# Attention's result in fp32, the first mixture's first layer on 64-row tiles, the loop written out, and new instruction orders

## The reference

```
x = x + attention(ln_c(x))          # q, k, v; softmax over d of q, over n of k; context; Wout
t = t + LN(moe0(ln_t(t)) + ln_t(t)) # router per IMAGE: mean of tokens, top 2 of 8 experts, gelu
x = x + conv3x3(ln_c(x), sign weights x mean|w|)
t = t + moe1(ln_t(t))               # all 8 experts, gelu, weighted per TOKEN by its top 2 gates
```

## Time and profile before

| | us |
|---|---|
| median of 3 runs | 429.95 (429.81 to 431.31) |
| profiled execution, whole | 429.15 |
| its span, first to last instruction | 427.4 |
| PE busy | 367.0 (86%) |
| DVE busy | 298.1 (70%) |
| ACT busy | 256.2 (60%) |
| POOL busy | 102.2 (24%) |

### The profile page before, as it was taken

How to read it: one execution, slowest core, us unless ns; L and a number is a source line. 1 busy time by engine, 2 the same in 40 slices (tenths; PEclk the granted TensorE clock), 3 DMA queues, 4 the chain that set the end, 5 groups by cost and what they waited for, 6 DMA issues and landing times.

```text
span 427.4 us, 6147 instructions
## 1 busy us (share of the span) xinstructions
PE 367.0 (86%) x1847; PEld 197.8 (46%) x1847; DVE 298.1 (70%) x691; ACT 256.2 (60%) x521; POOL 102.2 (24%) x93
## 2 busy tenths in 40 slices
PE   3869889899817465789999999999999998999994
PEld 3457676777704244354454444444444433433321
DVE  2498889998541545748778778778788788577442
ACT  2346557585635524458678678678678557557543
POOL 5226465656610313013013013012022021010000
PEclk9699999999966966679999999999999999999999
DMA  6930000000000000000010010010010010010101
GB/s 152 175 100 7 9 34 2 2 2 1 2 1 0 2 0 1 0 0 2 1 26 1 0 26 1 2 25 1 0 25 0 0 25 2 0 25 2 25 2 26
DMA packets 15947, 7.46 MB, mean 17 GB/s; under 512 B 14160, under 2 KB 14416, under 8 KB 15920
## 3 DMA queue, kind: packets, MB, share of 16 engines
q1 hardware_dynamic: 15920, 7.13, 8.4%
HBM read 5.03 MB, written 2.10 MB: 17 GB/s over the span
## 4 chain that ended last, share of the span: by engine, by line
PE 59%; DVE 17%; issue 11%; ACT 6%; POOL 2%; DMA 2%; POOLq 0%; ACTq 0%; DVEq 0%; SPq 0%
PE ps L787 13%; PE ps L816 11%; PE ps L739 6%; PE ps L694 4%; PE ps L797 4%; PE ps L709 3%; ACT HB L1432 2%; DVE qsum L995 2%; PE ps L615 2%; PE ps L763 2%; PE ps L808 1%; PE ps L527 1%; PE ps L574 1%; PE ps L724 1%; POOL rstdA L444 1%
## 5 line engine op out<-in xcount | busy, mean ns | idle before, releaser
L1226 DVE TENSOR_TENSOR XC<-HB,ps 128x512 f32<-128x512 f32 x128 | 83.6, 683 | 44.5 <-PE ps L797 26.4
L1432 ACT ACTIVATE HB<-ps,B1B 128x512 f32<-128x512 f32 x128 | 82.3, 683 | 42.6 <-PE ps L787 40.7
L787 PE MATMUL ps<-ET,W1B 64*128 64x512 f32 x256 | 71.1, 632 | 3.5 <-ACT HB L1432 3.0
L816 PE MATMUL ps<-XC,W2B 128*64 128x512 f32 x256 | 67.2, 613 | 0.4 <-DVE XC L1226 0.4
L444 POOL TENSOR_TENSOR rstdA<-varA,pow_half 128x8 f32<-128x8 f32 x16 | 26.2, 1638 | 139.4 <-DVE varA L917 139.4
L797 PE MATMUL ps<-CWTB,SEL 64*128 64x512 f32 x128 | 36.8, 570 | 2.6 <-DVE XC L1226 2.6
L444 POOL TENSOR_TENSOR rstd<-var,pow_half 128x4 f32<-128x4 f32 (+1 forms) x24 | 29.4, 1229 | 30.8 <-DVE var L917 30.3
L787 PEld LDWEIGHTS ps<-ET,W1B 64*128 64x128 f32 x256 | 20.6, 187 | 28.2 <-ACT HB L1432 15.3
L444 POOL TENSOR_TENSOR rstdB<-varB,pow_half 128x8 f32<-128x8 f32 x8 | 13.1, 1637 | 84.5 <-DVE varB L917 84.5
L739 PE MATMUL ps<-VP,WC 128*128 128x512 f32 x96 | 30.6, 478 | 1.5 <-ACT CWTB L1425 0.8
L694 PE MATMUL ps<-UTR,W1S 128*128 128x512 f32 (+1 forms) x64 | 24.7, 488 | 6.8 <-ACT XC L1380 3.8
(11 more groups left out here) (221 smaller groups left out, 656.2 us busy)
## 6 DMA issues: line engine op xcount, KB each, us to landing
out<-W1stage SPq DMA_DIRECT2D x8, 256.0 KB, 2.9
XC<-in_x SPq DMA_DIRECT2D x6, 256.0 KB, 5.7
T<-in_x SPq DMA_DIRECT2D x1, 512.0 KB, 3.7
W1stage<-in_w1a SPq DMA_DIRECT2D x1, 512.0 KB
W1B<-in_w1b SPq DMA_DIRECT2D x1, 512.0 KB, 3.6
W1stage<-in_wconv SPq DMA_DIRECT2D x1, 288.0 KB, 2.7
W1stage<-in_wcs SPq DMA_DIRECT2D x1, 288.0 KB, 3.1
K<-in_consts SPq DMA_DIRECT2D x1, 266.0 KB, 2.8
```

Of the source, the lines that this page charges most:

```text
L787: mm(ps[:, H_BANK[c], :], W1B[half(c), e, :], ET[half(c), par, :], start=True, stop=True).then_inc(s["f_h"], 1)
L816: ins = mm(acc[c * C:(c + 1) * C, :], W2B[:, e, :], HG[:, (2 * e + c) % 4, :], start=False, stop=(e == E - 1), skip_group_check=True)
L1226: tt(HG[:, m % 4, :], HB[:, m % 2, :], ps[:, CW_BANK[m % 2], :], ALU.mult).then_inc(s["f_hg"], 1)
L1432: av(HB[:, m % 2, :], ps[:, H_BANK[m % 2], :], ACT.Gelu, bias=B1B[:, m // 2:m // 2 + 1])\
```

## The change

- The kernel keeps attention's result in fp32 only. `u_to_channels` is now two fp32 products of 128 x 129 in place of four fp32r transposes; its extra column is of ones and gives the sum over tokens. ACT copies it in one instruction into `UT`, where four had done copy and sum. The cast (DVE) and the subtraction (POOL) are gone.
- The first layer of the first mixture is multiplied in fp32 on 64-row tiles: `a_hidden` has 2 parts with 2 products each, one on the upper 64 rows of the array and one on the lower. They write two banks (A and V). The preparation of a split W1 is gone. The tokens of a unit are g and g+4 in place of neighbours.
- All periods are written out; there is no hardware loop.
- Both tables of orders are new.

```diff
 PLAN = dict(
     pool=(
-        "b_rstd-1 a_rstd1 a_rstd0+1"
+        "a_rstd0+2 a_rstd1+2 b_rstd+2"
...
-def periods(eng, plan, parts):
+def periods(plan, parts):
...
-    for b in range(-MOST_AHEAD, MOST_AHEAD):
-        period(b, b % 2, plan, parts, image_exists)
-    with eng.Fori(0, (B - 2 * MOST_AHEAD) // 2) as i:
-        for par in range(2):
-            period(eng.snap(2 * i + (MOST_AHEAD + par)), par, plan, parts, lambda name, b, ahead: True)
-    for b in range(B - MOST_AHEAD, B + MOST_AHEAD):
+    for b in range(-MOST_AHEAD, B + MOST_AHEAD):
         period(b, b % 2, plan, parts, image_exists)
...
-        W1A = sb("W1A", [P, E, 2, F], F32R)
+        W1A = sb("W1A", [P, E, F])
...
-            return (H_BANK + CW_BANK)[n] if early(b) else A_BANK
+            return (H_BANK + CW_BANK)[n] if early(b) else (A_BANK, V_BANK)[n % 2]
...
             def u_to_channels(g):
...
-                    pe.wait_ge(s["ulo"], n + 1)
+                    pe.wait_ge(s["u"], n + 1)
...
-                    for r in range(4):
-                        ins = pe.transpose(ps[:, UT_BANK, r * P:(r + 1) * P].bitcast(F32R),
-                                           US[:, n % 2, r].rearrange("p k c -> p (k c)"), ident_r[:, :])
+                    for i in range(2):
+                        ins = mm(ps[:, UT_BANK, i * (P + 1):(i + 1) * (P + 1)],
+                                 U[:, 2 * p + i, UT_ * g:UT_ * g + UT_, :].rearrange("p h c -> p (h c)"), IDS[:, :],
+                                 start=True, stop=True)
...
-            def a_hidden(n):
+            def a_hidden(k):
                 def part(b, par):
-                    k, c = n // 2, n % 2
-                    if c == 0:
-                        pe.wait_ge(s["a_sel"], 4 * b + 2 * k + 1)
+                    pe.wait_ge(s["a_sel"], 4 * b + 2 * k + 1)
                     if early(b):
-                        ge(pe, s["a_gelu"], 4 * (b - 1) + n + 1)
-                    elif n == 0:
-                        ge(pe, s["a_z"], b)
+                        ge(pe, s["a_gelu"], 4 * (b - 1) + 2 * k + 2)
+                    elif k == 0:
+                        pe.wait_ge(s["a_z"], b)
+                        pe.wait_ge(s["a_img"], 2 * b)
                     else:
-                        pe.wait_ge(s["a_gelu"], 4 * b + n)
-                    for w in range(2):
-                        ins = mm(ps[:, a_bank(n, b), :], W1S[:, k, w, :],
-                                 UTR[:, bass.ds(b, 1), c * HALF:(c + 1) * HALF].rearrange("p a n -> p (a n)"),
-                                 start=(w == 0), stop=(w == 1))
-                    ins.then_inc(s["a_h"], 1)
+                        pe.wait_ge(s["a_gelu"], 4 * b + 2)
+                    for c in range(2):
+                        mm(ps[:, a_bank(2 * k + c, b), :], W1S[half(c), k, :],
+                           UT[half(c), bass.ds(b, 1), :, 0:P].rearrange("p a j n -> p (a j) n"),
+                           start=True, stop=True).then_inc(s["a_h"], 1)
...
-                    vec.tensor_copy(US[:, k, :, 0, :].rearrange("p (j b) c -> p b j c", b=2),
-                                    U[:, 2 * p:2 * p + 2, UT_ * g:UT_ * g + UT_, :]).then_inc(s["uhi"], 1)
...
-                    for i in range(2):
-                        ins = av(UTR[:, 2 * p + i, UT_ * g * P:UT_ * (g + 1) * P].rearrange("p (j n) -> p j n", n=P),
-                                 src[:, :, i, :], ACT.Copy, accum_out=usum[:, 2 * p + i, g:g + 1])
-                    ins.then_inc(s["uT"], 1)
+                    src = ps[:, UT_BANK, 0:2 * (P + 1)].rearrange("p (b n) -> p b n", b=2)
+                    av(UT[:, 2 * p:2 * p + 2, g, :], src, ACT.Copy).then_inc(s["uT"], 1)
```

More of the change, by code:

```diff
@@ L821, in _ @@
             pe.wait_ge(s["set_dve"], SET_F1)
-            periods(pe, PLAN["pe"], dict(
+            periods(PLAN["pe"], dict(
                 [(f"f_hidden{e}", f_hidden(e)) for e in range(E)]
-                    + [(f"a_hidden{n}", a_hidden(n)) for n in range(4)]
+                    + [(f"a_hidden{k}", a_hidden(k)) for k in range(2)]
                     + [("a_output", a_output), ("a_z_turned", a_z_turned), ("a_vT0", a_vT(0)), ("a_vT1", a_vT(1)),
```

98 lines of the change are left out of this document (42 added, 56 removed), and 25 rows, old and new, of tables (act, pe, vec).

## The result

The changed kernel takes 445.62 us (median of 4 runs, 444.52 to 446.69) against 430.63 for the kernel before on the same chip (4 runs, 429.81 to 431.81): ratio 1.0346, interval 1.0306 to 1.0385. It is slower, as forecast, but the loss is 15.0 us where 7 was forecast: inside the wide range (426 to 447), and above 443, the upper end of the forecast's own. The profiled execution has a span of 442.7 us (444.52 as a whole) against 427.4.

What follows compares the result with a forecast made beforehand. PE's work bounds the periods, a chain of dependent steps the filling. Attention -6.5, filling +13.0, first image and five periods +5.0, end -4.0 sum to +7.5 on 429.15; with half of 0.8 added, 437 us, range 431 to 443, wide 426 to 447.

Steps and rivals of the forecast that it cites:

- Attention: Attention: cast, subtraction, copies, reads and W1 split go, PE's part stays; -6.5 us, bounds 0 and -11.
- The filling: Before the first `f_hidden`: two stage-a chains run one after the other, delaying it by 13.0 us; bounds +9 and +17.
- PE's work per period: TensorE's list in one loop period: 31.45 less 0.63 and 0.38, plus 0.4, gives 30.85 us.
- The wait: Each period: PE stands 1.2 us before `f_hidden3` for ACT, DVE adds 0.35; period 32.4 us against 31.45.
- Rival C: Periods: DVE bounds, `f_output7` waits behind `b_normalise` and `a_zn`; 33.3 us per period, 2 more for fill, 443.5 us; chance 0.18.
- The first image: First image's `f_start`, at a clock just coming up: +0.3 us.
- The end: Where stages a and b run out: fewer PE waits, 70.5 us against 74.5, so -4.0; bounds -7 and 0.
- Rival A: Periods: `f_hidden3` finds its bank free, period 30.85 us, total 429.5, no change; chance 0.15.
- B: Attention pays in full, -11 us, with periods of 30.85 and filling +9: 421 us; chance 0.12.

Runs made afterwards that it cites:

- the third combined run: Changed kernel with re-ordered filling, exp and top 2 moved for images 1 to 6, image 1's `b_gates_turned` and image 2's two `a_vT` placed later: 430.33 us.
- both joined forms: Old mixture orders, `a_hidden` joined to two parts: the kernel before in fp32r, 428.95 us, and the changed kernel in 64-row fp32, 423.05 us.

## Why the forecast was right in sign and half in size

- **Attention, -6.5.** The total held (-6.6), its working did not. I counted instructions that go; the run with the old orders shows the same arithmetic 12 to 16 us later without its order table. How the gain divides between the two is open. The ranges above put it between 3.8 and 13.0, so the agreement to 0.1 is luck.
- **The filling, +13.0.** Right in mechanism and place, measured +14.7. The walk held up to the convolution of image 1, which comes at 178.61 (forecast 184.9, less the 6.5 of attention, so 178.4). From its end to `f_hidden` I summed 9.3 and it took 10.5. The order table is the whole cause: to the second `f_start` it takes 88.0 with the old table and the new arithmetic, 108.2 with the new table and the old arithmetic. Of the 21.1 between the changed kernel and the old table, 4.4 is image 1's first layer behind image 0's `a_vT`; the same for image 2, with image 0's experts earlier, brought 3.9 more. Another profile of that last order gives 2.2 more still, so these shares are good to some 2 us. How the other 10.6 to 12.8 divide among image 2's norm, image 1's gates and the half clock is open: my idea that `b_gates_turned` of image 1 sets them fell in the third combined run.
- **"PE's work per period", 30.85.** This step failed. The list needs 31.7 with the new orders as they are (32.88, the mean of the four full steps, less one chain of 1.2), and 31.1 with the top 2 moved (31.40 less 0.27 of idle). I credited 0.63 to the 64-row tiles and 0.38 to gates beside hidden layers, against an estimate of 0.4 for other neighbours. The two parts of `a_hidden` did cost the 1.93 forecast (1.06, and 1.29 with the gate behind). But of the seven pairs of gate and hidden layer only three take the 1.29 that I gave to each: the two whose gates wait, for experts 6 and 7, take 1.67 and 1.56, the one split by the wait of `f_hidden3` 1.55 beside that wait, and the one ahead of `b_gates` 1.43. That is 1.05 a period, more than the whole error. Nor was the 0.63 a gain of the tiles as such: in the same new order one expert's two halves in joined fp32r take 1.00 us, a pair of 64-row fp32 tiles 1.06:

```profile
318.93 1.17 PE L688 MATMUL ps<-UTR,W1S 128*128 128x512 f32 x4
319.93 3.22 PE L733 MATMUL ps<-VP,WC 128*128 128x512 f32 x12
322.99 1.09 PE L688 MATMUL ps<-UTR,W1S 128*128 128x512 f32 x4
324.01 0.51 PE L791 MATMUL ps<-CWTB,SEL 64*128 64x512 f32 x2
```

  and the neighbours pay: `a_hidden` and the gate behind it take 1.46 here and 1.29 in the changed kernel, but the convolution steps 3.06 here and 3.22 there. The step is 32.67 with the old arithmetic and 32.8 to 33.1 with the new, so retyping costs 0.2 in the mean; with the old orders both joined forms give 31.68. The Trainium skill ("TensorEngine Tiling (Array Packing)", "Theoretical Speedup") allows up to a factor 2; these rows show none against fp32r on 128 rows, as 1.06 stands against 1.00.
- **The wait, 1.2 + 0.35.** The 1.18 of `f_hidden3` was exact; the 0.35 did not come on top. I took VectorE's as a small addition to ScalarE's, while the two run beside each other and each is enough alone. Rival C, priced at 443.5, was nearest in the total. It was right that VectorE bounds, and wrong in the place: not `f_output7` but the stretch from `b_gates` to `b_gates_turned`.
- **The first image, +0.3.** The first `f_start` comes 5.40 us after the first `f_hidden`, 4.49 before: +0.9. The first step is 34.15, 1.3 above the mean of the next four: the granted clock was 0.95 in it, after 0.70 through the filling. Before, it was 0.93 up to the first `f_start` and 1.00 from there on, and the first step (31.30) was no longer than the others. In the sum I had no term for a first step at a lower clock.
- **The end, -4.0.** Measured -2.5: the steps to the last `f_start` are 30.65 and 22.91 (before 30.53 and 25.34), and the tail behind it is unchanged, 24.23 and 24.42. I had summed 29.6 and 21.9 for the two steps, 1.0 too little for each, and 0.5 too much behind them.
- Rival A (no waits) and B (attention in full, filling +9) did not come.

The miss of 7.8 in the sum is 4.7 from the periods, 1.7 from the filling and 1.5 from the end. The 4.7 are 0.48 in each of five steps (TensorE's list 0.83 too short, less the 0.35 of the wait that did not come), 1.3 in the first step, 0.6 up to the first `f_start`, and 0.4 because the five steps before average 31.37 and not 31.45.
